# A four-layer graph network: destination rows gathered inside the second edge stage, its instruction orders rewritten, accumulate rounds and stores moved between stages

## The reference, cut to what matters

```python
# layer 2, continuous filter; src, dst are the ends of the edges
h = x @ W_in2f
Wij = (shifted_softplus(f_ij @ W_f1 + b_f1) @ W_f2 + b_f2) * rcut_ij[:, None]
y = segment_sum(h[idx_j] * Wij, idx_i, num_segments=N_ATOMS)
out = shifted_softplus(y @ W_o1 + b_o1) @ W_o2 + b_o2
# layer 3, two mean-aggregating convolutions
mean = agg / jnp.maximum(cnt, 1.0)[:, None]
return mean @ Wl.T + bl + x @ Wr.T
# in the last two layers idx_i = src and idx_j = dst; layer 3 averages x[src] over each dst
```

## Time and profile before

| | us |
|---|---|
| median of 3 runs | 2704.23 (2695.72 to 2710.38) |
| the profiled execution | 2708.5 |
| its span, first to last instruction | 2706.7 |
| stage ef, about | 1131 to 1410 |
| stage al | 1410 to 1996 |
| stage em | 1996 to 2385 |
| stage el | 2385 to 2707 |

### The profile page before, as it was taken

One profiled execution on the slowest core, in us unless ns is written; L12 is line 12 of the kernel. 1 busy time (PEld: TensorE's weight loads), 2 busy tenths in 40 slices (PEclk: granted clock), 3 DMA queues, 4 the chain that ended last, 5 costly groups with the idle time before them and its releaser, 6 DMA issues. The chain is left out here.

```text
span 2706.7 us, 46999 instructions
## 1 busy us (share of the span) xinstructions
PE 2196.2 (81%) x14558; PEld 1837.3 (68%) x14558; DVE 1966.6 (73%) x2890; ACT 1781.0 (66%) x3704; POOL 1629.1 (60%) x1214
## 2 busy tenths in 40 slices
PE   5999999999979999788938986898868888724443
PEld 4999999999967777566627775777746666523332
DVE  5999999999966666487828995888858989723332
ACT  4888888888856777565616774777758888711111
POOL 5887767777314443268875557888703433368887
PEclk9999999999989999798969998999989999965555
DMA  4666655555448888668846776888736666543332
GB/s 99 157 141 159 140 156 148 144 151 141 135 136 227 256 250 255 173 170 213 209 108 147 164 160 161 218 228 225 217 106 196 204 199 196 151 112 96 105 100 60
DMA packets 338765, 447.31 MB, mean 165 GB/s; under 512 B 121523, under 2 KB 177673, under 8 KB 338520
## 3 DMA queue, kind: packets, MB, share of 16 engines
q1 hardware_dynamic: 218216, 380.39, 49.0%
q0 software_dynamic: 120000, 63.45, 13.1%
q10 hardware_dynamic: 304, 0.49, 0.1%
HBM read 252.29 MB, written 192.56 MB: 164 GB/s over the span
## 5 line engine op out<-in xcount | busy, mean ns | idle before, releaser
L1644 POOL DMA_INDIRECT out<-em_c,to_s x100 | 135.8, 1358 | 291.3 <-DVE em_c L1960 265.4
L1593 POOL DMA_INDIRECT combined<-acc,idx x200 | 262.0, 1310 | 63.9 <-issue 60.7
L1574 POOL DMA_INDIRECT acc<-combined,first_ x100 | 211.6, 2116 | 121.1 <-DMA acc<-combined,first_ 67.0
L444 PE MATMUL banks<-mats,g_hT 128*125 128x256 f32 x1000 | 259.0, 382 | 0.0
L464 PE MATMUL banks<-mats,g_zT 128*125 128x128 f32 x2000 | 238.8, 273 | 0.0
L464 PEld LDWEIGHTS banks<-mats,g_zT 128*125 128x125 f32 x2000 | 228.1, 188 | 0.0
L737 POOL DMA_INDIRECT gin_xs<-x,from_ x100 | 126.7, 1267 | 161.6 <-DMA x_of_src<-gin_xs 137.6
L444 PEld LDWEIGHTS banks<-mats,g_hT 128*125 128x125 f32 x1000 | 189.3, 189 | 29.9 <-issue 0.4
L508 ACT ACTIVATE g_sq<-banks 125x512 f32<-125x512 f32 x250 | 148.1, 593 | 83.7 <-PE banks L444 83.5
L581 DVE TENSOR_REDUCE g_ss<-g_sq 125x4 f32<-125x1024 f32 x125 | 151.4, 1211 | 66.6 <-ACT g_sq L508 66.6
L525 ACT ACTIVATE g_zT<-banks,cols 128x500 f32<-128x500 f32 x250 | 178.8, 775 | 1.5 <-PE banks L452 1.5
(11 more groups left out here) (355 smaller groups left out, 7016.1 us busy)
## 6 DMA issues: line engine op xcount, KB each, us to landing
x<-g_x SPq DMA_DIRECT2D x125, 224.0 KB
g_x<-in_xT SPq DMA_DIRECT2D x100, 250.0 KB
acc<-g_zero SPq DMA_DIRECT2D x101, 224.0 KB
gin_x<-x SPq DMA_DIRECT2D x50, 448.0 KB
h<-gin_hr SPq DMA_DIRECT2D x50, 448.0 KB
al_h<-h SPq DMA_DIRECT2D x50, 448.0 KB
al_x<-x SPq DMA_DIRECT2D x50, 448.0 KB
out<-al_out SPq DMA_DIRECT2D x50, 448.0 KB
```

What stands on the lines that cost most here:

```text
L444: m = nc.tensor.matmul(bank[0:P, 256 * j:256 * j + 256], HT[q % 2][:, c:c + P], K.W1c, start=False, stop=j == 1)
L1574: pool.indirect_dma_start(out=K.acc, out_offset=bass.IndirectOffsetOnAxis(ap=K.first[:, g, r:r + 1], axis=0), in_=CR[:, g, r * D:r * D + D ...
L1593: pool.indirect_dma_start(out=CR[:, m % 6, r * D:r * D + D], out_offset=None, in_=K.acc, in_offset=bass.IndirectOffsetOnAxis(ap=idx[:, g, ...
L1644: pool.indirect_dma_start(out=out, out_offset=bass.IndirectOffsetOnAxis(ap=K.to_s[:, k, r:r + 1], axis=0), in_=C[k % 4][:, r, :], in_offse ...
```

## The change

1. ROUNDS goes from 10 to 6: four accumulate rounds move from stage ef into the start of POOL's list in stage al, which has 19 now.
2. The gathers of `y` at the destinations leave stage al, with the table `y_of_dst`, its stores and its loads. In stage em POOL gathers these rows from `acc` straight into em_yd (four buffers in place of three), one group ahead of each scatter; a scatter stands at lag 5 of POOL's list.
3. In stage al, SP keeps the first gathered group at step 27 in place of 20.
4. The orders of PE, ACT and DVE in stage em are new; `apply_c` comes at lag 2 in place of 3.
5. The stages of nodes_alone become methods of a class `Nodes`, with the same instructions in the same order.

```diff
-        ROUNDS = 10
+        ROUNDS, PAIRS = 6, NG // 2
...
-                    for m in range(2 * EG):
-                        if 20 + (3 * m) // 5 == i:
+                    for m in range(tables * EG):
+                        if 27 + (3 * m) // 5 == i:
                             keep(sp, m)
...
-        for m in range(2 * EG):
-            idx, _, g = of(m)
+        for m in range(EG):
             past_slot(pool, kept, m - 6, 32)
...
             def _(pool):
-                for k in range(EG):
+                def get(k):
+                    past(pool, ydT, k - 4)
+                    for r in range(R):
+                        pool.indirect_dma_start(out=YD[k % 4][:, r, :], out_offset=None, in_=K.acc,
+                                                in_offset=bass.IndirectOffsetOnAxis(ap=K.dst[:, k, r:r + 1], axis=0)).then_inc(got[k % 4], 16)
+
+                def put(k):
                     past(pool, done, k)
                     past_slot(pool, sent, k - 1, 16 * R)
...
+                steps(EG, [(0, get), (5, put)])
...
-                    past(sp, ydT, k - 3)
-                    move(sp, flat(YD[k % 3]), slots_of(K.yd, k), din[k % 3])
...
                 def turn_yd(k):
-                    past_slot(pe, din, k, 80)
+                    past_slot(pe, got, k, 16 * R)
...
-                steps(EG, [(0, turn), (0, turn_y), (1, turn_x3), (0, first), (0, turn_back), (1, hidden), (0, turn_yd), (0, first_d),
-                           (1, back_h), (1, turn_x3d), (1, second), (0, update), (1, hidden_d), (0, update_d), (1, back_hd)])
+                steps(EG, [(0, turn), (0, turn_y), (0, turn_back), (1, turn_x3), (0, first), (0, turn_yd), (1, hidden), (1, turn_x3d),
+                           (0, first_d), (1, back_h), (1, second), (0, update), (1, hidden_d), (0, update_d), (1, back_hd)])
...
-                steps(EG, [(1, apply_b), (1, nbd.reduce_of(dve)), (3, apply_c), (1, sums), (0, residual), (0, positive), (1, apply_bd),
-                           (1, average), (0, na.reduce_of(dve)), (0, soft), (0, positive_d), (0, apply_a), (0, join), (0, soft_d),
-                           (1, residual_c), (0, nb.reduce_of(dve)), (0, join_d), (1, rows_hd), (1, nc_.reduce_of(dve))])
+                steps(EG, [(1, apply_b), (1, nbd.reduce_of(dve)), (0, residual), (1, apply_bd), (1, sums), (0, positive), (1, average),
+                           (2, apply_c), (0, na.reduce_of(dve)), (0, soft), (0, positive_d), (0, apply_a), (1, residual_c), (0, join),
+                           (0, soft_d), (1, nc_.reduce_of(dve)), (0, nb.reduce_of(dve)), (0, join_d), (1, rows_hd)])
```

More of the change, by code:

```diff
@@ L1115, in halves, with __init__ @@
     return tile[:, :, :].rearrange("p (h r) d -> p h (r d)", h=2)
[L1118 to L1123, removed]
+class Nodes:
+    def __init__(self, nc, K, out, name, ctx, first, count, banks):
         def sb(n, shape, dt=F32, k=2):
@@ L1128, in sem @@
             return K.sem(f"{name}_{n}")
[L1130 to L1141, removed]
+        self.nc, self.K, self.table, self.begin, self.count = nc, K, out, first, count
+        self.pH, self.pA, self.pX, self.pU, self.pC = banks
+        self.X, self.H, self.OUT = [sb(n, [P, 2 * R, D], k=3) for n in ("x", "h", "out")]
@@ new lines, in log_c, with exp_c, residual @@
+    def log_c(self, act, k):
+        if k < self.count:
+            self.nc_.log(act, k)
+    def exp_c(self, act, k):
+        if k < self.count:
+            self.nc_.exp(act, k, self.done)
+    def residual(self, dve, k, h):
+        if k < self.count:
+            t = 2 * k + h
+            past(dve, self.back, t)
+            past_slot(dve, self.xin, k, 64)
+            past(dve, self.b, k - 2)
+            self.nc.vector.scalar_tensor_tensor(out=self.half(self.A[k % 2], h), in0=self.half(self.X[k % 3], h), scalar=2.0,
+                                                in1=banked(self.pA[h % len(self.pA)]), op0=ALU.mult, op1=ALU.add).then_inc(self.a, 1)
@@ L1143, in nodes_alone, with on @@
+def on(stage, eng, *h):
+    return lambda k: stage(eng, k, *h)
+def nodes_alone(nc, K, out, count, side, keep, kept_all, tables):
+    ctx = ExitStack()
+    with ctx:
+        n = Nodes(nc, K, out, "al", ctx, 0, count, (K.ps[0], K.ps[1:3], K.ps[3:5], K.ps[5], K.pairs[3]))
         with nc.Block() as block:
@@ L1147, in _ @@
             def _(sp):
[L1148 to L1160, removed]
+                for i in range(count + 4):
+                    n.load(sp, i)
@@ L1170, in _ @@
             @block.tensor
             def _(pe):
[L1172 to L1218, removed]
+                steps(count, [(0, on(n.turn, pe, 0)), (0, on(n.turn, pe, 1)), (2, on(n.hidden, pe, 0)), (0, on(n.turn_back, pe, 0)),
+                              (0, on(n.turn_back, pe, 1)), (2, on(n.hidden, pe, 1)), (2, on(n.second, pe, 0)), (2, on(n.second, pe, 1)),
+                              (1, on(n.turn_x3, pe, 0)), (1, on(n.turn_x3, pe, 1))])
```

237 lines of the change are left out of this document (164 added, 73 removed).

## The result

The changed kernel takes 2631.02 us, the median of 3 runs (2625.04 to 2632.16), against 2704.23 before: a ratio of 0.9726 with a 95% interval of 0.9678 to 0.9774. The forecast was 2628 (2603 to 2657).

The account below looks back on a forecast made before the run. POOL's tail was taken to bound ef, SP's list against POOL's speed al, and a handover loop em. Gains of 32.9 + 20 + 23 = 76 us took the profiled 2708.5 to 2632, as a median 2628 us, range 2603 to 2657.

Parts of the forecast that it names:

- The forecast loop: Em: handovers from residual through soft_d, update_d, back_hd, turn, relu_b and turn_back set the step, 13.2 us for 13.89.
- Ef, 32.9: End of ef: four fewer accumulate rounds let al begin at 1377.2, 32.9 us earlier.
- POOL's last gather would end at 1365: End of ef: four fewer rounds take 38.7 us from POOL, so its last gather ends before ACT's 1375.7.
- So ACT sets the end: End of ef: ACT, done at 1375.7, finishes last; 1.5 us for the engines' meeting puts al at 1377.2.
- POOL or its last store still is last: End of ef: lower bound of the gain, 28 us, if POOL's tail still ends the stage.
- Al, 20: Al: four more rounds, keep seven steps later and half the groups win 20 us, between 5 and 30.
- Its wait falls from 22.7 to 9.8 us: Al: SP's wait at its first keep shrinks as it arrives at 277.7 for a group ready at 287.5; 12.9 won.
- Em, 23: Em: 15.9 us won by shorter steps and 10 at the end, 3 lost at the start.
- POOL's gathers at nothing: Em: 100 more POOL issues, 13.1 us of issues a step, cost nothing, covered up to about 1.9 us issue to issue.
- The price of an issue beside VectorE: Em: POOL issues beside a busy VectorE priced from measured rows, gathers 1.31 and scatters 1.36 us, not the skill's 3,100 ns.
- one term fails: Rival: em stays at 13.89 or al's loss stays, giving 2643 to 2659 us; 0.24 for one or two terms failing.

Follow-up runs that it names:

- e1: Changed kernel with ten accumulate rounds in ef again, in place of six: 2656.9 us, ef 280.2 us.
- e2: Changed kernel with SP's keep starting at step 20 of al in place of 27: 2699.6 us, al 622.3 us.
- e3: Changed kernel with the old PE, ACT and DVE orders in em, POOL's new gathers kept: 2653.4 us, em step 13.89 us.
- e6: Changed kernel with turn_back behind turn_x3 and first again in TensorE's em list: 2729.8 us, em step 14.92 us.
- e9: Changed kernel with apply_c behind soft_d in VectorE's em order and without em's scatters: 2608.2 us, em step 13.07 us.
- e8: Changed kernel with a fifth, unread gather per group in em, so nine POOL issues a step: 2712.0 us, em step 14.81 us.
- e10: Changed kernel with em's four scatters a step replaced by five unread gathers: 2636.8 us, em step 13.14 us.
- e5: Changed kernel without em's hundred scatters of em_c, POOL issuing only gathers there: 2658.8 us, em step 13.14 us.
- e11: The same kernel as e8, run a second time: 2657.8 us, em step 14.12 us, ratio 0.9802 to the kernel before.
- e12: Changed kernel with ef's keep_h one step later from group 14 and apply_c behind soft_d in em: 2640.53 us, ratio 0.9726 to the kernel before.

## Why the prediction was right, point by point

- **What bounds each stage** held. POOL's tail in ef (e1), SP's list in al (e2) and a loop of handovers in em (e3, e6) each answer to the one edit that touches them. The forecast loop is the one that binds, but another lay only 0.3 us under it (e9), which the forecast did not look for.
- **Ef, 32.9**: mis-sized, 25.7 in the profile. The step that failed is "POOL's last gather would end at 1365". It ended at 1378.3, since POOL waited 11.4 us in four places for stores of h_of_src to land, where before it waited for no such store (rows above, 1359.56). "So ACT sets the end" failed with it. Over the ten kernels with this ef, POOL's last gather ends 236.6 to 247.0 us after the stage's start, where the forecast was 233, and ACT's last `combined` 239.3 to 253.1 after, where it was 243.8. In eight of them al begins 6.1 to 6.3 us after POOL's last gather, the time that its landing, SP's last store and that one's landing took before too; in the other two (e8, e10) it begins 1.1 us after ACT's last `combined`. So POOL's tail still sets the end in most, though by little. The mean of ef is 249.2, which is 29 won. The forecast's own bound for "POOL or its last store still is last" was 28.
- **Al, 20**: mis-sized, 27.6. "Its wait falls from 22.7 to 9.8 us" failed to the good side: it fell to nothing. Rounds took (1646.66 - 1385.23 - 6.84) / 18 = 14.1 us each and not 14.8. So the gathers began 270.2 us after the first round, and the first group was there when SP came at 281.9, where the forecast had 287.5. From store 16 to store 46 315.5 us went by, a loss of 6.8 to the 308.7 of the pairs alone, where 18.6 was left in the forecast. The first stores come 3 us later than before. E2's 63.8 us is what the old step 20 would have cost.
- **Em, 23**: right, 25.3. The 23 steps from the second em_a on gave 17.7 for 15.9. The start cost nothing for 3: the first `turn_yd` came 1.1 us later, but the second em_a stands 24.5 us after the first load, where it was 24.7. The end, from the last em_a to el, gave 7.4 for 10 (44.8 to 37.4). Of the parts of the end, em_c came 1.4 sooner and the four issues less gave 6.0. The wait for the group before to land stayed at 3.0 us but began before the last em_c was done, so 1.6 of it was still paid, where the forecast had it gone. And el began 6.0 us after the last issue, 1.3 more than before.
- **POOL's gathers at nothing**: right as to the time, for e5 has the same step without the scatters. The argument was incomplete. It said that four groups of lead cover POOL up to 1.9 us an issue. E10 bears that out and e8 doesn't: with nine issues, 14.8 us of POOL a step, the step grew at once. The covering buffers weren't what gave way.
- **The price of an issue beside VectorE** was rightly taken from the rows. Most issues took 1.19 to 1.23 us beside a VectorE that is 93% busy, the others 1.30 to 1.91. The Trainium skill ("SBUF — State Buffer", section "SBUF: two separate sides" and the one after it) says that GpSimd can't write a DMA's descriptors while VectorE holds the port that they share, and gives 3,100 ns for a DMA beside a copy. The trace agrees in so far as issues that begin beside certain instructions of VectorE are 0.1 to 0.7 us longer (last section), and no run shows 3,100 ns; em's only copy, em_hrd, reads PSUM, so the page's case does not come up.
- **The range**: the rival "one term fails" didn't come, and errors of +7 and -8 cancelled. Terms mis-sized by a quarter to a third, with a sum right to a us, are luck in part.

## What to carry to other kernels

Read each stage at its own end, and for each waiting queue write down two times: when it gets to the wait, and when what it waits for is there. Moving work to another stage is free only where the first stays behind the second, which here took seven steps of SP's list and was worth 64 us. Where several engines are near 90%, follow the loop that comes back to itself after one step and add its pieces start to start; that gave the period within 0.1 us. Do it for the second loop too, since it sets how much the next edit can win: 0.06 of 0.68 us here. When a tail is cut, ask what its engine will wait for at the new pace, and carry the landing behind its last issue along (6.2 us here).

## What was not expected of the hardware

- A POOL issue that begins while VectorE is in an instruction with two inputs from SBUF (the scan, or a product like em_c with em_nc_r) is the long one. One from the changed kernel, instruction and issue:
```profile
2088.97 0.69 DVE L2035 TENSOR_TENSOR em_c<-em_c,em_nc_r 125x512 f32<-125x512 f32 x1
2089.16 1.58 POOL L1711 DMA_INDIRECT em_yd<-acc,idx  x1 [0.30 <-issue]
```
  The issue ends 1.08 us after that instruction, and the one at 2073.88 (above) 1.02 us after the scan. Between the second em_a and the last, 44 issues of the changed kernel begin so, at least 0.04 us after the start of such an instruction and 0.18 before its end; they take 1.30 to 1.91 us and end 1.01 to 1.11 us after the instruction. The other 128 take 1.19 to 1.23. In the kernel before and e10 the same split gives 1.47 to 1.64 against 1.19 to 1.20, and 1.30 to 1.94 against 1.21 to 1.22. No experiment moved an instruction to try it, so this is a coincidence in time and not a proven cause.
- Handovers from TensorE that come 0.6 to 1.5 us late, most of them 0.1 to 0.25 us behind the end of a POOL issue (e8, e11, one step of e12), with no semaphore of POOL's in them. Nine gathers a step without scatters don't show them.
- The same stage with the same instructions varies from run to run by more than the last edits at issue: ef 242.8 to 254.2 us in ten kernels. The changed al took 554.5 to 563.4 us in seven kernels, and 566.8 to 579.6 in e5 to e8, on the chip where the kernel before took 2771.56. A gain of 4 us in one stage can't be read off single profiles.
